# Value bias seeded by ScalarE, and one of four softmax sums a chunk prepared on GpSimd

## The chip, the cores and the metric

The kernel runs on one core of one Trainium2 chip. The metric is the device time of one execution in microseconds (us). The kernel before takes 356.97 us, the median of three runs (356.93 to 358.93).

## The reference, cut to what matters

The input x has 128 sequences of 64 tokens with 128 features, ctx a context of the same shape. First comes a cross-attention with 16 heads of 8 features, whose softmax goes over the heads, not over the keys:

```python
k = split_heads(ctx @ Wk.T + bk); q = split_heads(layernorm(x) @ Wq.T + bq)
v = split_heads(ctx @ Wv.T + bv)                 # [B, 16, S, 8]
score = einsum("bhij,bhkj->bhik", k, q) / sqrt(8)
attn = softmax(score, axis=1)                    # over the 16 heads
out = einsum("bhik,bhij->bhjk", attn, v)
x = x + merge(out) @ Wo.T + bo
x = x + ffn(layernorm(x))                        # three blocks of two dequantised layers, with low-rank parts
```

For each pair of a key and a query, then, 16 exponentials are summed and each is divided by the sum.

## The kernel before, in words

The 8192 tokens make 16 chunks of 512 tokens; a chunk is 8 sequences, in four pairs of two (p = 0 to 3). The cross-attention of all chunks runs first (some 225 us), the feed-forward phase behind it, with the first of its steps laid between the last chunks. The order on each engine is written out by hand; chunks 2 to 11 are a loop of two chunks a turn, the others are unrolled. Engines meet only through semaphores, and each engine works strictly in its own written order.

For each pair the work goes like this:

- TensorE, `scores` (L1441): 16 small products into `score_ps0` or `score_ps1`, turn about: 16 heads x 64 queries for the keys of two sequences. It signals `s_scores`.
- VectorE, `negmax` (L840): the negative maximum over the heads, 128x64 from 128x1024.
- TensorE, the shift (L1590): two products of 128x512 that add this maximum to the scores.
- ScalarE, `probs` (L1156): the exponentials of 128x1024, signalled by `s_exp`.
- VectorE, `zsum` (L858): the sum over the 16 heads, then `rz` (L861), its reciprocal.
- GpSimd, `probs` (L527): the exponentials times the reciprocal, in place, signalled by `s_probs`. There are four buffers `probs0` to `probs3`, one for each pair of a chunk, each with 8 bands of 64 x 2: the bands are the head pairs.
- TensorE, `att_ps` (L1647): 32 products of the weights with the block-diagonal values `v_diag`. Pair p of a chunk is used two quarters after its scores are shifted: pairs 0 and 1 in the quarters p = 2 and p = 3 of the same chunk, pairs 2 and 3 in p = 0 and p = 1 of the next.

On TensorE a quarter p begins with the scores of pair p+1, then comes the shift of pair p, then one piece of the projections for a later chunk (p=0: context and input turned, L1453 and L1459; p=1: queries, L1465 and their remainder L1485; p=2: keys, L1471 and L1491; p=3: the values of the next chunk, `project_v`, L1478), a part of the output projection (L1429) and the product with the weights. So the scores of pair 2 open quarter p=1.

`project_v` begins with `bias_rows` (L1413, `head_major=True`), a product of 128x512 that writes the value bias into the PSUM bank `work0`; the four value products (two records each) are added to it. ScalarE copies the result to `v_diag` (L1075).

GpSimd also computes, in quarter p=1 between the weights of pair 0 and of pair 1, the variance and its root for the input norm three chunks on (`input_variance`, L489 to L495, and `input_scale`, L476). VectorE computes the statistics for it (L618) in quarter p=1 behind the maximum of pair 1, and adds the attention's output to x (L774) in quarter p=3.

Of the kernel before, what the change touches and what calls it, by code (L numbers as in the profile page):

```python
# [9 lines left out]
ALU = mybir.AluOpType  # L10
ACT = mybir.ActivationFunctionType
AX_X = mybir.AxisListType.X
AX_XY = mybir.AxisListType.XY
# [6 lines left out]
P = 128  # L20
# [3 lines left out]
ADJ = 2  # L24
# [41 lines left out]
def build(nc, x, ctx_in, wk, bk, wq, bq, wv, bv, wo, bo, qw, qs, qb, la, lb, gamma, beta, out):  # L66
# [7 lines left out]
    with ExitStack() as es:  # L74
        def sb(name, shape, dt=F32):
            return es.enter_context(nc.sbuf_tensor(name, shape, dt))
# [4 lines left out]
        def sem(name):  # L81
            return es.enter_context(nc.semaphore(name))
# [17 lines left out]
        wq_c = sb("wq_c", [P, P])  # L100
        w_t = {k: sb("w_t_" + k, [P, P]) for k in "qkv"}
        wo_split = sb("wo_split", [P, 2, 2, P])
        wo_t = sb("wo_t", [P, 2, 2, P])
        cols = sb("cols", [P, NROWS])
        cols_h = sb("cols_h", [P, NROWS])
# [34 lines left out]
        v_diag = [sb(f"v_diag{i}", [P, PPC * HEADS * 32]) for i in range(2)]  # L140
        negmax = [sb(f"negmax{i}", [P, SEQ], BF16) for i in range(2)]
        probs = [sb(f"probs{i}", [P, BANDS, SEQ, ADJ]) for i in range(4)]
        zsum = [sb(f"zsum{i}", [P, SEQ]) for i in range(2)]
        rz = [sb(f"rz{i}", [P, SEQ]) for i in range(4)]
        att_t = [sb(f"att_t{i}", [P, 2, CHUNK // 2]) for i in range(2)]
# [72 lines left out]
        h_stack, h_k_stack = sem("h_stack"), sem("h_k_stack")  # L218
        h_q_out = [sem(f"h_q_out{u}") for u in range(2)]
        s_v_ps = sem("s_v_ps")  # L220
        s_v = sem("s_v")
        s_att_t = sem("s_att_t")
        s_wo = sem("s_wo")
# [3 lines left out]
        s_negmax = sem("s_negmax")  # L227
        s_shifted = sem("s_shifted")
        s_exp = sem("s_exp")
        s_zsum = sem("s_zsum")  # L230
        s_rz = sem("s_rz")
        s_probs = sem("s_probs")
# [20 lines left out]
        def live(c):  # L253

            return not isinstance(c, int) or 0 <= c < NCHUNK

        def some(count):

            return not isinstance(count, int) or count > 0
# [23 lines left out]
        def moments_slot(c):  # L283

            return 2 if isinstance(c, int) and c == 0 else 1

        def later(t):

# [177 lines left out]
        def _(pool):  # L466
# [18 lines left out]
            def input_variance(k):  # L485
# [10 lines left out]
                pool.wait_ge(s_aggr, 3 * k - 6)  # L496
                input_scale()

            def clear(tensor, done):

                for i in range(4):
                    ins = nc.gpsimd.memset(tensor[:, 512 * i:512 * (i + 1)], 0.0)
                ins.then_inc(done, 1)
# [13 lines left out]
            def chunk(c, par, half):  # L517
                for p in range(PPC):
                    n = PPC * c + p
                    mc = c - (p == 0)  # L520
                    if live(mc):
                        m = n - 1

                        pool.wait_ge(s_rz, m + 1)
                        e = probs[(p - 1) % 4]
                        by_query = rz[(p - 1) % 4][:, :].unsqueeze(1).unsqueeze(3)
                        nc.gpsimd.tensor_tensor(e[:, :, :, :], e[:, :, :, :],  # L527
                                                by_query.broadcast_to([P, BANDS, SEQ, ADJ]),
                                                ALU.mult).then_inc(s_probs, 1)
                    if p == moments_slot(c) and live(c + 3):  # L530
                        input_variance(c + 3)
                    input_part(X_VARIANCES, c, p, input_variances)
                    input_part(X_SCALES, c, p, input_scales)
                    early_steps("POOL", c, p, step)
# [80 lines left out]
        def _(dve):  # L615
# [214 lines left out]
                residual_columns()  # L830

            def chunk(c, par, half):
                for p in range(PPC):
                    n = PPC * c + p
                    if live(c):

                        dve.wait_ge(s_scores, n + 1)
                        if some(n - 1):
                            dve.wait_ge(s_shifted, n - 1)
                        nc.vector.tensor_reduce(negmax[p % 2][:, :],  # L840
                                                score_ps[p % 2][:, :].rearrange("p (h k) -> p k h", k=SEQ),
                                                AX_X, ALU.max, negate=True).then_inc(s_negmax, 1)
                    if p == moments_slot(c) and live(c + 3):
                        if not isinstance(c, int) or c + 3 >= 4:
                            dve.wait_ge(s_xnext[1 - par], 16 * (half + par))
                        else:
                            dve.wait_ge(s_xin[3], 16)
                        dve.wait_ge(s_rstd, c + 3)
                        input_stats_of(c + 3)
                    if p == 3 and isinstance(c, int) and c == NCHUNK - 2:  # L850
                        add_attention(c - 2)
                    mc = c - (p == 0)
                    if live(mc):

                        m = n - 1
                        q = (p - 1) % 2
                        dve.wait_ge(s_exp, m + 1)
                        nc.vector.tensor_reduce(zsum[q][:, :], probs[(p - 1) % 4][:, :, :, :].rearrange("p u k s -> p k u s"),  # L858
                                                AX_XY, ALU.add).then_inc(s_zsum, 1)
                        dve.wait_ge(s_zsum, m + 1)  # L860
                        nc.vector.reciprocal(rz[(p - 1) % 4][:, :], zsum[q][:, :]).then_inc(s_rz, 1)  # L861
                    if p == 3 and live(c - 2) and not (isinstance(c, int) and c == NCHUNK - 2):
                        add_attention(c - 2)
                    if isinstance(c, int) and (c, p) == (1, 0):
                        dve.wait_ge(s_res, 1)
                    input_part(X_STATS, c, p, input_stats_ahead)
                    early_steps("DVE", c, p, step)
                    if isinstance(c, int) and (c, p) == (NCHUNK, 0):
                        third_step()
                    if isinstance(c, int) and (c, p) == (NCHUNK, 3):  # L870
                        step_stats(4, 0)
                    if isinstance(c, int) and (c, p) == (NCHUNK + 1, 3):
                        step_sums(4, 0)
# [119 lines left out]
        def _(act):  # L993
# [12 lines left out]
            def early_layers():  # L1006

                act.wait_ge(s_lint_ps, 1)
                nc.scalar.activation(lin_t[:, 1:3, :].rearrange("p l d -> p (l d)"), att_ps[:, P:3 * P],
                                     ACT.Copy).then_inc(s_lint, 1)  # L1010
# [54 lines left out]
            def k_low(k, par):  # L1065
# [2 lines left out]
                nc.scalar.activation(parts[par][:, 1, 1, :], work1[:, :], ACT.Identity,  # L1068
                                     bias=cols_h[:, ROW_BK:ROW_BK + 1]).then_inc(s_k_lo, 1)

            def value_blocks(k, par, src=work0):

                for b in range(2):
                    dst = v_diag[par][SEQ * b:SEQ * (b + 1), :].rearrange("p (u a e) -> p u a e", a=4, e=16)
                    ins = nc.scalar.activation(  # L1075
                        dst[:, :, 0:4:3, DH * b:DH * (b + 1)],
                        src[SEQ * b:SEQ * (b + 1), :].rearrange("p (u s j) -> p u s j", s=2, j=DH), ACT.Copy)
                ins.then_inc(s_v, 1)
# [71 lines left out]
            def chunk(c, par, half):  # L1150
# [29 lines left out]
                if live(c + 2):  # L1180
                    q_high(c + 2, par)
                    if isinstance(c, int) and c == 0:
                        early_layers()
                    q_low(c + 2, par)
                if isinstance(c, int) and c == 0:
# [17 lines left out]
                if live(c + 2):  # L1203
                    k_high(c + 2, par)
                    if isinstance(c, int) and c == 0:
                        one_layer(4, 2)
                    k_low(c + 2, par)
                for u in range(2):
                    input_part(X_SCALED[u], c, 2, lambda t, u=u: input_scaled(t, u))
                early_steps("ACT", c, 2, step)  # L1210
# [140 lines left out]
        def _(pe):  # L1351
# [121 lines left out]

            def project_v(par, dst=work0):

                bias_rows(dst[:, :], 0, head_major=True)
                for q in range(PPC):
                    ins = nc.tensor.matmul(dst[:, TILE * q:TILE * (q + 1)], ctx_tr[par][:, TILE * q:TILE * (q + 1)],  # L1478
                                           w_t["v"][:, :], start=False, stop=True, skip_group_check=True)
                ins.then_inc(s_v_ps, 1)  # L1480
# [84 lines left out]
            def chunk(c, par, half):  # L1565
                for p in range(PPC):
# [15 lines left out]
                    if isinstance(c, int) and c == 0 and p == 0:  # L1582
                        pe.wait_ge(s_pick, 2 + len(BIAS_ROWS))
                        pe.wait_ge(s_split, 7)
                        project_v(0, wo_ps)

                    if live(c):
# [13 lines left out]
                    if p == 2 and live(c + 2):  # L1601
                        project_k(c + 2, par)
                    if p == 3 and live(c + 1):
                        if live(c + 2):
                            pe.wait_ge(s_q_lo, c + 3)
                        else:
                            pe.wait_ge(s_v, c + 1)
                        project_v(1 - par)

                    if isinstance(c, int) and (c, p) == (NCHUNK - 1, 3):  # L1610
# [278 lines left out]
```

## Time and profile before

| what | value |
|---|---|
| median of three runs | 356.97 us |
| profiled execution | 357.28 us, of it the span 355.5 us |
| granted TensorE clock, mean | 1.000 of full speed |
| TensorE busy | 340.4 us (96%) |
| VectorE busy | 325.9 us (92%) |
| ScalarE busy | 289.9 us (82%) |
| GpSimd busy | 266.1 us (75%) |

The span is the time from the first to the last instruction; the time outside it is the start and end of the program. Busy times are those of instructions alone. The profile names each instruction by its line (L527), its engine (PE is TensorE, PEld its weight loads, DVE VectorE, ACT ScalarE, POOL GpSimd) and the buffers that it writes and reads, without their numbers. Matmuls overlap each other, and their ends are modelled.

### The profile page before, as it was taken

To read this page: it belongs to the slowest core of one execution; us is meant where nothing else is said; L and a number is where in the kernel's file an instruction comes from. 1 tells how busy PE (TensorE), PEld (TensorE's weight loads), DVE (VectorE), ACT (ScalarE), POOL (GpSimd) and SP (SyncE) were. 2 spreads that over 40 slices of the span, in tenths; PEclk is the share of its full clock that TensorE was granted. 3 is DMA by queue.
4 is the path that set the end of the run, shared out by engine and by line. 5 is a ranking of instruction groups with operands and counts; after the bars stand their busy time and mean duration, and the time that the engine had idled before them with its cause. 6 is when DMAs were issued, how large, how long until landed. Compare 5 with 4: busy or idle time off the path is not lost.

```text
span 355.5 us, 13101 instructions
## 1 busy us (share of the span) xinstructions
PE 340.4 (96%) x4807; PEld 255.3 (72%) x4807; DVE 325.9 (92%) x818; ACT 289.9 (82%) x597; POOL 266.1 (75%) x283
## 2 busy tenths in 40 slices
PE   8979999999999999999999989999999999999995
PEld 7445477667667667766766767867888888888874
DVE  7879999999999999999999999978999999988774
ACT  4678888888878878888887878588989999999982
POOL 6537888877977987987799898878777778774231
PEclk9999999999999999999999999999999999999999
DMA  7989566659548746854944500000100001110112
GB/s 199 237 254 258 153 191 207 190 140 264 173 131 228 202 137 192 229 163 139 266 137 126 158 4 2 2 2 2 32 30 30 30 30 48 43 32 30 44 47 89
DMA packets 54530, 43.29 MB, mean 122 GB/s; under 512 B 4624, under 2 KB 48608, under 8 KB 54496
## 3 DMA queue, kind: packets, MB, share of 16 engines
q1 hardware_dynamic: 53920, 42.31, 41.0%
q10 hardware_dynamic: 576, 0.53, 0.5%
q8 instruction: 21, 0.34, 0.4%
q14 instruction: 13, 0.11, 0.1%
HBM read 26.05 MB, written 16.78 MB: 120 GB/s over the span
## 4 chain that ended last, share of the span: by engine, by line
PE 67%; POOL 10%; DVE 9%; ACT 4%; issue 4%; DMA 4%; SPq 1%; DVEq 0%; POOLq 0%; ACTq 0%
PE score_ps L1690 9%; POOL probs L527 7%; PE att_ps L1647 7%; PE score_ps L1590 6%; PE wo_ps L1429 5%; PE score_ps L1441 4%; PE score_ps L1793 3%; PE work L1465 3%; PE work L1786 3%; PE att_ps L1793 3%; PE work L1478 3%; PE work L1471 2%; PE score_ps L1684 2%; DVE st L884 2%; DVE zsum L858 2%
## 5 line engine op out<-in xcount | busy, mean ns | idle before, releaser
L527 POOL TENSOR_TENSOR probs<-probs,rz 128x1024 f32<-128x1024 f32 x64 | 136.3, 2140 | 27.9 <-DVE rz L861 27.8
L570 POOL TENSOR_TENSOR rs<-ve,minus_half 128x4 f32<-128x4 f32 (+1 forms) x47 | 55.6, 1183 | 33.7 <-DVE ve L786 24.3
L858 DVE TENSOR_REDUCE zsum<-probs 128x64 f32<-128x1024 f32 x64 | 77.4, 1209 | 2.5 <-ACT probs L1156 2.5
L1156 ACT ACTIVATE probs<-score_ps 128x1024 f32<-128x1024 f32 x64 | 65.6, 1025 | 13.0 <-PE score_ps L1590 12.2
L840 DVE TENSOR_REDUCE negmax<-score_ps 128x64 bf16<-128x1024 f32 x64 | 75.1, 1175 | 1.1 <-PE score_ps L1441 1.1
L1429 PEld LDWEIGHTS wo_ps<-wo_t,att_t 128*128 128x128 f32 x256 | 37.0, 191 | 13.4 <-issue 12.0
L1647 PE MATMUL att_ps<-probs,v_diag 128*32 128x64 f32 x2048 | 43.3, 224 | 1.2 <-POOL probs L527 0.8
L1252 ACT ACTIVATE z<-score_ps,rs 128x128 f32<-128x128 f32 x152 | 43.5, 382 | 1.1 <-POOL rs L570 1.1
L1690 PEld LDWEIGHTS score_ps<-lin_t,h 128*128 128x128 f32 x304 | 36.9, 191 | 9.9 <-DVE h L937 6.8
L1690 PE MATMUL score_ps<-lin_t,h 128*128 128x128 f32 x304 | 39.6, 278 | 1.3 <-DVE h L937 0.8
L1647 PEld LDWEIGHTS att_ps<-probs,v_diag 128*32 128x32 f32 x2048 | 32.8, 108 | 11.1 <-POOL probs L527 2.8
L1590 PE MATMUL score_ps<-negmax,ident_bf 128*128 128x512 bf16 x128 | 38.7, 384 | 1.3 <-DVE negmax L840 1.2
L1429 PE MATMUL wo_ps<-wo_t,att_t 128*128 128x128 f32 x256 | 38.3, 275 | 0.0
L861 DVE RECIPROCAL rz<-zsum 128x64 f32<-128x64 f32 x64 | 35.4, 553 | 2.2
L884 DVE BATCH_NORM_STATS2 st<-score_ps 128x6 f32<-128x128 f32 x152 | 33.8, 284 | 3.5 <-PE score_ps L1690 2.5
L1441 PE MATMUL score_ps<-q_stack,k_stack 64*64 64x128 f16 x1024 | 26.5, 222 | 2.5 <-DMA q_stack<-q_parts 1.6
L1441 PEld LDWEIGHTS score_ps<-q_stack,k_stack 64*64 64x64 f16 x1024 | 16.6, 106 | 13.9 <-issue 11.2
L476 POOL TENSOR_TENSOR half_rstd<-veps,minus_half 128x4 f32<-128x4 f32 x16 | 16.5, 1031 | 5.8 <-DVE veps L630 2.4
L1023 ACT ACTIVATE xln<-x_all,half_rstd 128x128 f32 (+1 forms) x60 | 19.0, 391 | 0.4 <-POOL half_rstd L476 0.4
L1786 PEld LDWEIGHTS work<-lin_t,g 128*128 128x128 f32 x104 | 13.7, 192 | 6.2 <-issue 6.2
L1263 ACT ACTIVATE g<-score_ps,cols 128x512 f32<-128x512 f32 x21 | 16.8, 798 | 1.4 <-PE score_ps L1684 1.4
L1075 ACT ACTIVATE v_diag<-work 64x512 f32<-64x512 f32 x30 | 17.6, 585 | 0.3
(275 smaller groups left out, 692.7 us busy)
## 6 DMA issues: line engine op xcount, KB each, us to landing
q_parts<-parts SPq DMA_DIRECT2D x15, 512.0 KB, 3.6
k_stack<-k_parts SPq DMA_DIRECT2D x30, 256.0 KB, 3.4
q_stack<-q_parts SPq DMA_DIRECT2D x60, 128.0 KB, 3.3
x_all<-in_x SPq DMA_DIRECT2D x16, 256.0 KB, 3.9
ctx_sb<-in_ctx SPq DMA_DIRECT2D x16, 256.0 KB, 3.7
k_parts<-parts SPq DMA_DIRECT2D x16, 256.0 KB, 3.0
out<-x_all SPq DMA_DIRECT2D x15, 256.0 KB, 2.3
q_parts<-parts SPq DMA_DIRECT2D x4, 128.0 KB, 2.3
```

What stands on the lines that cost most here:

```text
L527: nc.gpsimd.tensor_tensor(e[:, :, :, :], e[:, :, :, :], by_query.broadcast_to([P, BANDS, SEQ, ADJ]), ALU.mult).then_inc(s_probs, 1)
L570: nc.gpsimd.tensor_tensor(rs2[v][:, lo:hi], ve2[v][:, lo:hi], minus_half[:, lo:hi], ALU.pow).then_inc(p_rs[v], 1)
L840: nc.vector.tensor_reduce(negmax[p % 2][:, :], score_ps[p % 2][:, :].rearrange("p (h k) -> p k h", k=SEQ), AX_X, ALU.max, negate=True).the ...
L858: nc.vector.tensor_reduce(zsum[q][:, :], probs[(p - 1) % 4][:, :, :, :].rearrange("p u k s -> p k u s"), AX_XY, ALU.add).then_inc(s_zsum, 1)
L884: ins = nc.vector.bn_stats(st2[v][:, lo + i, :], src[:, TILE * i:TILE * (i + 1)])
L1156: nc.scalar.activation(probs[p][:, :, :, :], score_ps[p % 2][:, :].rearrange("p (u s k) -> p u k s", s=ADJ, k=SEQ), ACT.Exp, scale=SCALE). ...
L1252: ins = nc.scalar.activation(z[v][0][:, t, :], src[:, TILE * t:TILE * (t + 1)], ACT.Copy, scale=rs2[v][:, lo + t:lo + t + 1])
L1429: ins = nc.tensor.matmul(wo_ps[:, TILE * t:TILE * (t + 1)], att[:, o, TILE * u:TILE * (u + 1)], wo_t[:, o, b, :], start=False, stop=o == 1 ...
L1441: ins = nc.tensor.matmul(score_ps[mp % 2][SEQ * b:SEQ * (b + 1), c0:c0 + 2 * SEQ], k_stack[mb][half_rows, grp, k0:k0 + SEQ], q_stack[mb][h ...
L1590: ins = nc.tensor.matmul(score_ps[p % 2][:, CHUNK * o:CHUNK * (o + 1)], ident_bf[:, :], negmax[p % 2][:, :].unsqueeze(1).broadcast_to([P, ...
L1647: ins = nc.tensor.matmul(att_ps[32 * grp:32 * (grp + 1), c0:c0 + SEQ], v_diag[mb][:, v0:v0 + 32], probs[mp][:, band(hd), :, hd % ADJ], sta ...
L1690: ins = nc.tensor.matmul(dst[:, TILE * t:TILE * (t + 1)], hk[:, TILE * t:TILE * (t + 1)], lin_t[:, 2 * v - 2, :], start=v == 1 and t == 0, ...
```

## The change

Two things change.

The value bias: ScalarE reads the bias row once into SBUF (`value_row`, in chunk 0, from a product of 128 columns that TensorE puts into a free part of `att_ps`), and from then on copies it in each chunk, four times side by side, into `work0` (`value_seed`), between the two parts of the keys. `project_v` adds its products to that; the bias product goes, but for chunk 0's values, which are written to `wo_ps`.

The sum of pair 0: in chunks 1 to 12 GpSimd divides the weights of pair 3 of the chunk before in two halves of four bands, and between the halves adds the upper eight heads of pair 0's exponentials to the lower eight (`half_sum`, 128x512). VectorE sums eight instead of sixteen values for this pair, and takes the maximum of pair 2 ahead of this sum; in its old place that maximum is left out.

```diff
@@ -140,6 +141,7 @@
         probs = [sb(f"probs{i}", [P, BANDS, SEQ, ADJ]) for i in range(4)]
+        half_sum = sb("half_sum", [P, BANDS // 2, SEQ, ADJ])
@@ -283,6 +287,10 @@
+        def halved(c):
+
+            return not isinstance(c, int) or 1 <= c <= 12
@@ -496,6 +504,11 @@
+            def weigh(e, by_query, lo, hi):
+
+                return nc.gpsimd.tensor_tensor(e[:, lo:hi, :, :], e[:, lo:hi, :, :],
+                                               by_query.broadcast_to([P, hi - lo, SEQ, ADJ]), ALU.mult)
@@ -524,9 +537,14 @@
                         by_query = rz[(p - 1) % 4][:, :].unsqueeze(1).unsqueeze(3)
-                        nc.gpsimd.tensor_tensor(e[:, :, :, :], e[:, :, :, :],
-                                                by_query.broadcast_to([P, BANDS, SEQ, ADJ]),
-                                                ALU.mult).then_inc(s_probs, 1)
+                        if p == 0 and halved(c):
+                            weigh(e, by_query, 0, BANDS // 2)
+                            pool.wait_ge(s_exp, n + 1)
+                            nc.gpsimd.tensor_tensor(half_sum[:, :, :, :], probs[0][:, 0:BANDS // 2, :, :],
+                                                    probs[0][:, BANDS // 2:BANDS, :, :], ALU.add).then_inc(s_half, 1)
+                            weigh(e, by_query, BANDS // 2, BANDS).then_inc(s_probs, 1)
+                        else:
+                            weigh(e, by_query, 0, BANDS).then_inc(s_probs, 1)
@@ -830,16 +848,25 @@
+                def maxima(p):
+
+                    n = PPC * c + p
+                    dve.wait_ge(s_scores, n + 1)
+                    if some(n - 1):
+                        dve.wait_ge(s_shifted, n - 1)
+                    nc.vector.tensor_reduce(negmax[p % 2][:, :],
+                                            score_ps[p % 2][:, :].rearrange("p (h k) -> p k h", k=SEQ),
+                                            AX_X, ALU.max, negate=True).then_inc(s_negmax, 1)
+
+                def head_sums(q, src):
+
+                    nc.vector.tensor_reduce(zsum[q][:, :], src.rearrange("p u k s -> p k u s"), AX_XY,
+                                            ALU.add).then_inc(s_zsum, 1)
...
-                    if live(c):
...
+                    if live(c) and not (halved(c) and p == 2):
+                        maxima(p)
@@ -854,9 +881,13 @@
-                        dve.wait_ge(s_exp, m + 1)
-                        nc.vector.tensor_reduce(zsum[q][:, :], probs[(p - 1) % 4][:, :, :, :].rearrange("p u k s -> p k u s"),
-                                                AX_XY, ALU.add).then_inc(s_zsum, 1)
+                        if p == 1 and halved(c):
+                            maxima(2)
+                            dve.wait_ge(s_half, c)
+                            head_sums(q, half_sum[:, :, :, :])
+                        else:
+                            dve.wait_ge(s_exp, m + 1)
+                            head_sums(q, probs[(p - 1) % 4][:, :, :, :])
@@ -1067,6 +1098,22 @@
+            def value_bias():
+
+                act.wait_ge(s_value_row, 1)
+                nc.scalar.activation(value_row[:, :], att_ps[:, 0:P], ACT.Copy).then_inc(s_value_row, 1)
+
+            def value_seed(k):
+
+                if live(k + 1):
+                    act.wait_ge(s_q_lo, k + 2)
+                else:
+                    act.wait_ge(s_v, k)
+                if isinstance(k, int) and k == 1:
+                    act.wait_ge(s_value_row, 2)
+                nc.scalar.activation(work0[:, :].rearrange("p (q d) -> p q d", q=PPC),
+                                     value_row[:, :].unsqueeze(1).broadcast_to([P, PPC, P]), ACT.Copy).then_inc(s_v_seed, 1)
@@ -1204,7 +1252,10 @@
                     k_high(c + 2, par)
...
+                    value_seed(c + 1)
                     k_low(c + 2, par)
+                elif live(c + 1):
+                    value_seed(c + 1)
@@ -1473,7 +1524,6 @@
             def project_v(par, dst=work0):
 
-                bias_rows(dst[:, :], 0, head_major=True)
@@ -1582,6 +1632,9 @@
+                        nc.tensor.matmul(att_ps[:, 0:P], pick_row[:, 0, :], bias3_h[:, :], start=False, stop=True,
+                                         skip_group_check=True).then_inc(s_value_row, 1)
+                        bias_rows(wo_ps[:, :], 0, head_major=True)
                         project_v(0, wo_ps)
@@ -1601,10 +1654,7 @@
-                        if live(c + 2):
-                            pe.wait_ge(s_q_lo, c + 3)
-                        else:
-                            pe.wait_ge(s_v, c + 1)
+                        pe.wait_ge(s_v_seed, c + 1)
                         project_v(1 - par)
```

VectorE in the loop, quarter p=1 and the beginning of p=2 of one chunk, before. `stats` are those of a later chunk's input, `negmax0` is pair 2's maximum, `zsum0` and `rz0` belong to pair 0, `zsum1` to pair 1:

```order
L618 BN_STATS stats<-x_all 128x6
L858 TENSOR_REDUCE zsum0<-probs0 128x64
L861 RECIPROCAL rz0<-zsum0 128x64
L837 REGISTER_ALU
L840 TENSOR_REDUCE negmax0<-score_ps0 128x64
L858 TENSOR_REDUCE zsum1<-probs1 128x64
L861 RECIPROCAL rz1<-zsum1 128x64
```

The same place now:

```order
L636 BN_STATS stats<-x_all 128x6
L854 REGISTER_ALU
L857 TENSOR_REDUCE negmax0<-score_ps0 128x64
L863 TENSOR_REDUCE zsum0<-half_sum 128x64
L892 RECIPROCAL rz0<-zsum0 128x64
L863 TENSOR_REDUCE zsum1<-probs1 128x64
L892 RECIPROCAL rz1<-zsum1 128x64
```

Pair 2's maximum has moved ahead of pair 0's sum and reciprocal, and with it its wait for the scores of pair 2; the sum now reads `half_sum`.

GpSimd in the loop, from the weights of pair 3 to those of pair 0, before; the rows below them are the moments:

```order
L527 TENSOR_TENSOR probs3<-probs3,rz3 128x1024
L524 REGISTER_ALU
L527 TENSOR_TENSOR probs0<-probs0,rz0 128x1024
L487 REGISTER_ALU
L488 REGISTER_ALU
L489 TENSOR_TENSOR agg<-stats 128x4
```

And now:

```order
L509 TENSOR_TENSOR probs3<-probs3,rz3 128x512
L542 REGISTER_ALU
L543 TENSOR_TENSOR half_sum<-probs0 128x512
L509 TENSOR_TENSOR probs3<-probs3,rz3 128x512
L509 TENSOR_TENSOR probs0<-probs0,rz0 128x1024
L495 REGISTER_ALU
```

The addition stands between two halves of pair 3's weights. Pair 0, the moments and pair 1 follow each other as before.

## Rows read from the trace of the kernel before

**Rows 1.** The page: busy time, share of the span and instructions of each engine.

```profile
PE 340.4 (96%) x4807; PEld 255.3 (72%) x4807; DVE 325.9 (92%) x818; ACT 289.9 (82%) x597; POOL 266.1 (75%) x283
```

**Rows 2.** Window of chunk 6: us, busy PE, PEld, DVE, ACT, POOL; clock, DMA, GB/s.

```profile
101.15:113.80 12.65, 12.65 (x242) 8.87 (x242) 12.37 (x17) 10.42 (x17) 10.41 (x10) 1.00 0.65 186
```

**Rows 3.** The chain of waits in chunk 4: start us, us, what.

```profile
82.20 0.22 PE work L1413
```

**Rows 4.** TensorE in order of time, chunks 5 and 6: start us, us, instruction.

```profile
87.48 0.42 PE L1441 MATMUL score_ps<-q_stack,k_stack 64*64 64x128 f16 x16
...
94.61 0.38 PE L1413 MATMUL work<-bias_h,pick_row 128*128 128x512 bf16 x1
...
96.47 0.69 PE L1647 MATMUL att_ps<-probs,v_diag 128*32 128x64 f32 x32
...
97.58 0.61 PE L1590 MATMUL score_ps<-negmax,ident_bf 128*128 128x512 bf16 x2
...
100.20 0.42 PE L1441 MATMUL score_ps<-q_stack,k_stack 64*64 64x128 f16 x16
...
109.26 0.68 PE L1647 MATMUL att_ps<-probs,v_diag 128*32 128x64 f32 x32
...
112.85 0.42 PE L1441 MATMUL score_ps<-q_stack,k_stack 64*64 64x128 f16 x16
```

**Rows 5.** VectorE in order of time, chunk 5: pair 0, pair 2's maximum, pair 1.

```profile
87.28 1.20 DVE L858 TENSOR_REDUCE zsum<-probs 128x64 f32<-128x1024 f32 x1
88.52 0.55 DVE L861 RECIPROCAL rz<-zsum 128x64 f32<-128x64 f32 x1
88.99 1.16 DVE L840 TENSOR_REDUCE negmax<-score_ps 128x64 bf16<-128x1024 f32 x1
90.07 1.20 DVE L858 TENSOR_REDUCE zsum<-probs 128x64 f32<-128x1024 f32 x1
```

**Rows 6.** GpSimd in order of time, chunk 5: pair 0, then pairs 1 and 2.

```profile
89.15 2.14 POOL L527 TENSOR_TENSOR probs<-probs,rz 128x1024 f32<-128x1024 f32 x1 [1.41 <-DVE rz L861]
...
93.48 4.24 POOL L527 TENSOR_TENSOR probs<-probs,rz 128x1024 f32<-128x1024 f32 x2
```

**Rows 7.** Groups by form: form, count, busy us, mean ns, idle before; several stretches.

```profile
L594 POOL TENSOR_TENSOR z<-x_all,rs 128x512 f32<-128x512 f32 x13 | 13.5, 1040 | 0.0
...
L1293 ACT ACTIVATE score_ps<-seed 128x512 f32<-128x512 f32 x15 | 9.4, 624 | 0.0
...
L774 DVE TENSOR_TENSOR x_all<-wo_ps,x_all 128x512 f32<-128x512 f32 x2 | 1.3, 628 | 0.0
```

**Rows 8.** ScalarE in order of time, chunk 5: the two key copies.

```profile
92.74 0.70 ACT L1062 ACTIVATE parts<-work,cols_h 128x512 f16<-128x512 f32 x1
93.92 0.69 ACT L1068 ACTIVATE parts<-work,cols_h 128x512 f16<-128x512 f32 x1 [0.48 <-PE work L1491]
```

**Rows 9.** Order of time, two releases: TensorE to VectorE, GpSimd to TensorE.

```profile
233.99 1.13 PE L1690 MATMUL score_ps<-lin_t,h 128*128 128x128 f32 x8 [0.53 <-ACT lin_t L1015]
...
235.15 0.89 DVE L884 BATCH_NORM_STATS2 st<-score_ps 128x6 f32<-128x128 f32 x4 [0.65 <-PE score_ps L1690]
...
210.54 4.23 POOL L527 TENSOR_TENSOR probs<-probs,rz 128x1024 f32<-128x1024 f32 x2
...
212.72 0.69 PE L1647 MATMUL att_ps<-probs,v_diag 128*32 128x64 f32 x32 [0.84 <-POOL probs L527]
```

**Rows 10.** TensorE in order of time: pair 2's scores and pair 1's product, chunks 1, 12.

```profile
36.93 0.42 PE L1441 MATMUL score_ps<-q_stack,k_stack 64*64 64x128 f16 x16 [0.17 <-ACT probs L1156]
...
45.84 0.69 PE L1647 MATMUL att_ps<-probs,v_diag 128*32 128x64 f32 x32
...
176.11 0.42 PE L1441 MATMUL score_ps<-q_stack,k_stack 64*64 64x128 f16 x16
...
185.50 0.69 PE L1647 MATMUL att_ps<-probs,v_diag 128*32 128x64 f32 x32
```

**Rows 11.** TensorE in order of time, end of chunk 14: a shift that waits.

```profile
207.45 0.60 PE L1590 MATMUL score_ps<-negmax,ident_bf 128*128 128x512 bf16 x2 [0.54 <-DVE negmax L840]
```

More of the change, by code:

```diff
@@ L102, in build @@
         wo_split = sb("wo_split", [P, 2, 2, P])
+        value_row = sb("value_row", [P, P])
         wo_t = sb("wo_t", [P, 2, 2, P])
@@ L220, in build @@
         s_v_ps = sem("s_v_ps")
+        s_value_row, s_v_seed = sem("s_value_row"), sem("s_v_seed")
         s_v = sem("s_v")
@@ L229, in build @@
         s_exp = sem("s_exp")
+        s_half = sem("s_half")
         s_zsum = sem("s_zsum")
@@ L832, in chunk @@
             def chunk(c, par, half):
+                def maxima(p):
[9 more added lines that the diff above has]
+                                            ALU.add).then_inc(s_zsum, 1)
                 for p in range(PPC):
                     n = PPC * c + p
-                    if live(c):
[L837 to L842, printed above, removed]
+                    if live(c) and not (halved(c) and p == 2):
+                        maxima(p)
                     if p == moments_slot(c) and live(c + 3):
@@ L1182, in chunk @@
                     if isinstance(c, int) and c == 0:
+                        value_bias()
                         early_layers()
```

## The prediction

> **What bounds the kernel now.** I read the page first, then the window of a whole chunk, the chain of waits in another, and the order of time on each engine over chunks 5 and 6. The page says that no engine stands out: TensorE is busy 96% of the span and VectorE 92% [rows 1]. In chunk 6 TensorE is busy 12.65 of 12.65 us, VectorE 12.37, ScalarE and GpSimd 10.42 and 10.41, at the full granted clock, 2.4 GHz [rows 2]. The chain of waits runs through TensorE alone there, and the value bias product stands in it with 0.22 us [rows 3]. So TensorE sets the period, with VectorE some 0.3 us behind.
>
> The rest rests on distances, which I take on TensorE. Call S the end of the scores of pair 2 (start + 0.42 us). The product of pair 1's weights with the values, which ends the quarter p=3, is due 8.57 us after S in chunk 5 (96.47 - 87.90) and 8.64 in chunk 6 (109.26 - 100.62); from its start to the next S go 4.15 us (loop jump included) and 4.01 (113.27 - 109.26) [rows 4]. Together 12.72 and 12.65: two consecutive periods.
>
> GpSimd delivers pair 1's weights like this: reciprocal of pair 0 starts at 88.52 on VectorE, GpSimd weighs pair 0 from 89.15 (0.63 later), then computes the moments of a later chunk, then weighs pair 1 from 93.48 to 95.62 (half of 4.24) [rows 5, 6]. From 89.15 to 95.62 are 6.47 us. TensorE wants the result at 96.47, so 0.85 us are spare.
>
> **The change, part by part.**
>
> *TensorE, value bias.* One product of 0.22 us [rows 3] goes from each of 15 chunks. In chunk 0 there is one 128-column product more. Gain where TensorE bounds: 0.22 a chunk.
>
> *ScalarE, value seed.* One copy of 128x512 from SBUF into PSUM a chunk, 0.62 us by the seed copies of the later phase [rows 7]. It stands between the two key copies, where ScalarE now waits 0.48 us for the key remainder [rows 8]. So the low key part comes some 0.1 us later, and the seed is in PSUM near 94.1 (92.74 + 0.70 + 0.62), before TensorE begins on the values at 94.61 [rows 4]. Cost: 0. If the gap were gone, the exponential behind it would be up to 0.6 us late.
>
> *VectorE.* Pair 0's sum takes 8 x 64 elements instead of 16 x 64: the whole takes 1.20 us [rows 5]. No row shows the half. Below stands half of the whole, 0.60; VectorE's addition of 128x512 takes 0.63 [rows 7]; with the reduction's pattern I allow up to 0.75 and take 0.67, near the row of equal size. That frees 0.5 us a chunk. But the order moves: pair 2's maximum now stands ahead of pair 0's sum.
>
> *GpSimd.* The whole product of 2.14 us [rows 6] becomes two halves, and between them comes an addition of 128x512. Products of 128x512 take 1.04 [rows 7]: 2.08 + 1.04 = 3.12 instead of 2.14, so GpSimd's 10.4 become 11.4 of 12.7. As a share that fits. I take 1.04 for the addition; as bounds 0.5 (half of a 1.04) and 2.14. The addition needs pair 0's exponentials, whose shift TensorE ends 2.43 us before S (97.58 + 0.61 to 100.62 [rows 4]); with 0.1 to ScalarE, an exponential of 1.0, 0.1 to GpSimd and the addition it is done about 0.2 us before S. VectorE wants it 1.1 us after S. So the wait added on it costs nothing up to about 1.3 us more.
>
> *The new loop.* Pair 2's maximum cannot start before S. Behind it, in VectorE's own order, stand pair 0's sum and reciprocal, and for them waits GpSimd's whole row. After S:
> - to the start of the maximum: 0.03 us (a product ends at 235.12, VectorE starts at 235.15) [rows 9] to 0.08 (reciprocal ends 89.07, GpSimd starts 89.15 [rows 5, 6]); I take 0.05, near the row of VectorE itself
> - maximum to next start: 1.08 (88.99 to 90.07) [rows 5]
> - half sum 0.67, and 0.04 to the reciprocal as now (87.28 + 1.20 to 88.52): 0.71
> - reciprocal to GpSimd's start: 0.63
> - weigh pair 0, moments, weigh pair 1: 6.47
> - to TensorE: 0.05 (the first of the two products from 210.54 ends near 212.67, TensorE starts 212.72) [rows 9]
>
> Sum 8.99 us after S. TensorE's own way to that place is now 8.57 and 8.64, less the bias 8.35 and 8.42. It will stand still there some 0.6 us. And this does not pass: the next S comes 4.15 or 4.01 us behind that product [rows 4], so the loop closes, with 13.14 and 13.00 us. Against 12.72 and 12.65 that is +0.42 and +0.35 a chunk, with TensorE's saving already swallowed. Put otherwise: GpSimd begins pair 0 now 1.25 us after S (89.15 - 87.90), and would begin it 2.47 after S.
>
> *Sum.* Chunk 1: now 8.49 from S to the product (45.84 - 37.35) [rows 10], so +0.50. Chunks 2 to 11: five of each kind, 5 x 0.42 + 5 x 0.35 = 3.85. Chunk 12: now already 8.97 (185.50 - 176.53) [rows 10], because VectorE's statistics of the second phase come in; those start about 0.12 later, so +0.12. From chunk 13 VectorE and GpSimd have hardly a gap and TensorE waits for them (0.54 us for a maximum at 207.45 [rows 11]), so the two bias products that still fall away there win nothing, and GpSimd starts 1.2 us in arrear: I put +0.1. Together 0.50 + 3.85 + 0.12 + 0.10 = 4.57. The profiled execution took 357.28 us (span 355.5 and 1.8 around it), 0.3 over the median 356.97. So 361.85 in it, and 361.5 as the median.
>
> *A rule against this result.* The shares say that TensorE and VectorE are the fullest, at 96% and 92% [rows 1], and the change relieves both. The Trainium skill, "Perfetto Trace Analysis", section "Identifying the Most-Contended Engine", says to take the engine with the highest occupancy first (for TensorE it wants the weight loads' share instead of the matmuls', and then VectorE is first). By that rule this change should win: that is rival 1 below. The distances above say that a chain through all three engines becomes longer than any engine's row; whether it is so, no row of before can show.
>
> For the addition the skill's "GPSIMD Engine Reference", section 3.1, gives 2.6 cycles an element at 1.2 GHz for two inputs. By it 512 elements would be 1.1 us, an estimate, which would leave the sum as it is.
>
> **Rivals.**
>
> 1. *TensorE stays the bound* (the other side: faster). Then 12 chunks save 0.22 each: -2.6, 354.7 in the profiled execution, 354.3 as the median. For it: the busy shares, and 0.85 us spare behind GpSimd now. Against it: the delay of GpSimd's start is 1.22 us, and 0.85 less the 0.22 by which TensorE comes earlier are there to hide it. It decides where the way from S to the product gets under 8.4: the loop would have to be 0.6 us shorter than I make it.
> 2. *The loop bites, but is shorter.* The ends of matmuls are modelled, so the maximum could start 0.07 us earlier; the half sum could be 0.60, another 0.07; and while TensorE stands still, its queue could take in the loop jump, so that the 4.15 us in every second chunk become 4.01. That is 0.14 in 12 chunks and 0.14 in 5 more, 2.4 together: +2.2, 359.5 in the profiled execution, 359.2 as the median. For it speaks that each of these is possible at once; against it, that VectorE's row at 235.15 starts behind the modelled end and not before it [rows 9].
> 3. *GpSimd gets slower by the neighbour.* If its added work beside VectorE's reductions made each of its instructions 10% longer, 6.47 would be 7.1, and 12 chunks cost 7.6 more: 369. Against it: in chunk 5 the products have 2.14 and 2.12 us [rows 6], alone or beside VectorE's longest reductions.
>
> **How the numbers follow.** A measurement of this kernel tells about 1% from no change, 3.6 us. My forecast, 361.5, has 0.67, rival 1 has 0.10, rival 2 has 0.18, rival 3 has 0.05. The forecast's own range is 360.4 to 363.2 (0.03 to 0.08 at S is -0.2 and +0.4 over 12 chunks; the half sum between 0.60 and 0.75 is -0.8 and +1.0; the tail -0.1 to +0.5, and not all at one end). The whole range takes in rival 2 and leaves rival 1, rival 3 and the outer edges out: 358.8 to 363.8. Slower by over 1% (above 360.5): 0.60 of the forecast, 0.02 of rival 2 and rival 3, 0.67 together. Within 1%: 0.07 of the forecast, 0.16 of rival 2, and 0.06 of rival 1, whose 354.3 lies 0.7% under the median: 0.29. Faster by over 1% (under 353.4): the rest of rival 1, 0.04.
>
> **What would show it.** In the profile after: chunks 2 to 11 with a period near 13.07 us; on TensorE a repeated gap of some 0.6 us before the weights product, released by GpSimd's product; on VectorE a gap of about 1 us before pair 2's maximum, released by the scores; GpSimd starting pair 0 some 2.4 us after S; no gap of VectorE before the half sum; ScalarE's seed near 0.62 and no wait for it. Wrong would be the forecast if TensorE had no gap there and a period of 12.43, or if the gap's releaser were the seed or the addition.

## The result, and the profile after

The changed kernel takes 362.74 us (median of 4 runs, 362.21 to 363.36), the kernel before 356.95 in the runs beside it: ratio 1.0149, 95% interval 1.0111 to 1.0188. It is slower by 1.5%. The profiled execution took 362.78 us, 5.50 more than that of before.

The page of the changed kernel, busy time and two of its groups (line, engine, operation, count, busy, mean ns, idle time before and its releaser):

```profile
PE 338.2 (94%) x4793; PEld 253.9 (70%) x4793; DVE 321.4 (89%) x818; ACT 296.9 (82%) x613; POOL 282.2 (78%) x307
...
L857 DVE TENSOR_REDUCE negmax<-score_ps 128x64 bf16<-128x1024 f32 x64 | 76.2, 1192 | 12.4 <-PE score_ps L1492 12.3
...
L1697 PE MATMUL att_ps<-probs,v_diag 128*32 128x64 f32 x2048 | 43.3, 224 | 8.5 <-POOL probs L509 8.2
```

Against [rows 1] TensorE has 2.2 us less to do and VectorE 4.5 us less, and both are idle for a larger share of a longer span. The two groups say where: VectorE waits for scores before a maximum, TensorE for GpSimd's weights. The waits of the same kernel (engine, line waited for, us in all, times, longest) give the counts:

```profile
DVE negmax L857 <- PE score_ps L1492: 12.3, 15, 1.0
PE att_ps L1697 <- POOL probs L509: 8.2, 14, 0.8
DVE zsum L863 <- ACT probs L1203: 1.2, 3, 0.6
POOL half_sum L543 <- ACT probs L1203: 0.3, 1, 0.3
```

Of each of the first two about one a chunk. The third line is the sums on VectorE: they waited three times, for ScalarE, and never for the addition. So the addition is not what the loop waits for; it waited itself only once (the fourth line). Then TensorE in order of time (start us, us, instruction, idle before and its releaser): pair 1's product in the chunks 1, 2, 3, 5, 6 and 11 and the scores of pair 2 in 1, 4, 5 and 6; the scores at 99.37, those of pair 1 of chunk 6, are the first product behind the loop jump. They answer to [rows 4] and [rows 10].

```profile
36.60 0.42 PE L1492 MATMUL score_ps<-q_stack,k_stack 64*64 64x128 f16 x16
...
46.09 0.69 PE L1697 MATMUL att_ps<-probs,v_diag 128*32 128x64 f32 x32 [0.53 <-POOL probs L509]
59.16 0.68 PE L1697 MATMUL att_ps<-probs,v_diag 128*32 128x64 f32 x32 [0.56 <-POOL probs L509]
...
72.23 0.68 PE L1697 MATMUL att_ps<-probs,v_diag 128*32 128x64 f32 x32 [0.64 <-POOL probs L509]
...
75.97 0.42 PE L1492 MATMUL score_ps<-q_stack,k_stack 64*64 64x128 f16 x16
...
89.03 0.42 PE L1492 MATMUL score_ps<-q_stack,k_stack 64*64 64x128 f16 x16
...
98.51 0.68 PE L1697 MATMUL att_ps<-probs,v_diag 128*32 128x64 f32 x32 [0.64 <-POOL probs L509]
99.37 0.42 PE L1492 MATMUL score_ps<-q_stack,k_stack 64*64 64x128 f16 x16 [0.18 <-issue]
...
102.35 0.42 PE L1492 MATMUL score_ps<-q_stack,k_stack 64*64 64x128 f16 x16
...
111.81 0.68 PE L1697 MATMUL att_ps<-probs,v_diag 128*32 128x64 f32 x32 [0.54 <-POOL probs L509]
...
177.39 0.69 PE L1697 MATMUL att_ps<-probs,v_diag 128*32 128x64 f32 x32 [0.63 <-POOL probs L509]
```

The same gap stands before the same product in each of the chunks 1 to 11, 0.53 to 0.64 us. From S (89.03 + 0.42) to the product are 9.06 us, in chunk 6 (102.77 to 111.81) 9.04. From the product of chunk 1 to that of chunk 11 are 131.30 us, 13.13 a turn. Before, it was 45.84 [rows 10] to 172.54 in this row of the kernel before, so 126.70 us, 12.67 a turn:

```profile
172.54 0.68 PE L1647 MATMUL att_ps<-probs,v_diag 128*32 128x64 f32 x32
```

VectorE and GpSimd of the changed kernel over the same stretch of chunk 5; they answer to [rows 5] and [rows 6]:

```profile
89.50 1.23 DVE L857 TENSOR_REDUCE negmax<-score_ps 128x64 bf16<-128x1024 f32 x1 [0.97 <-PE score_ps L1492]
90.64 0.68 DVE L863 TENSOR_REDUCE zsum<-half_sum 128x64 f32<-128x512 f32 x1
91.36 0.55 DVE L892 RECIPROCAL rz<-zsum 128x64 f32<-128x64 f32 x1
```

```profile
87.46 1.17 POOL L509 TENSOR_TENSOR probs<-probs,rz 128x512 f32<-128x512 f32 x1
88.58 1.27 POOL L543 TENSOR_TENSOR half_sum<-probs 128x512 f32<-128x512 f32 x1
89.82 1.16 POOL L509 TENSOR_TENSOR probs<-probs,rz 128x512 f32<-128x512 f32 x1
91.99 2.14 POOL L509 TENSOR_TENSOR probs<-probs,rz 128x1024 f32<-128x1024 f32 x1 [1.02 <-DVE rz L892]
...
96.33 5.36 POOL L509 TENSOR_TENSOR probs<-probs,rz 128x1024 f32<-128x1024 f32 x3
```

Read the loop in these rows: S (the end of pair 2's scores) at 89.45, maximum 0.05 later, 1.14 to the half sum, 0.72 to the reciprocal, 0.63 to GpSimd at 91.99. Pair 1's weights begin at 96.33 and are done near 98.46 (6.47 behind 91.99, as before), TensorE starts 0.05 later, and 4.26 us on is the next S. These are the signs that the forecast named: the gap of 0.6, VectorE's wait of 1 us (0.97), GpSimd 2.54 us after S, a turn of 13.13 where it had 13.07. The addition ended near 89.85, 0.8 us before the half sum wanted it, and before the half sum VectorE has no gap.

### The profile page after: what moved, and what is told of

Same layout as the page of the kernel before. It is cut to its first block, busy times and chain, and to the rows that moved or that the text cites. A ratio compares the mean times of both kernels' runs of the same rounds, so it can differ in the third digit from the quotient of the medians.

```text
span 361.0 us, 13114 instructions
## 1 busy us (share of the span) xinstructions
PE 338.2 (94%) x4793; PEld 253.9 (70%) x4793; DVE 321.4 (89%) x818; ACT 296.9 (82%) x613; POOL 282.2 (78%) x307
## 4 chain that ended last, share of the span: by engine, by line
PE 33%; POOL 31%; issue 23%; DVE 6%; ACT 3%; DMA 2%; POOLq 1%; SPq 0%; ACTq 0%; DVEq 0%
POOL probs L509 20%; PE score_ps L1740 9%; POOL half_sum L543 4%; PE score_ps L1843 3%; PE work L1836 3%; PE att_ps L1843 3%; PE score_ps L1734 2%; DVE st L915 2%; PE wo_ps L1740 1%; PE att_ps L1734 1%; PE work L1734 1%; PE work L1826 1%; DMA k_stack<-k_parts 1%; POOL half_rstd L484 1%; ACT probs L1203 1%
## 5 line engine op out<-in xcount | busy, mean ns | idle before, releaser
L509 POOL TENSOR_TENSOR probs<-probs,rz 128x1024 f32<-128x1024 f32 (+1 forms) x76 | 137.9, 1829 | 16.8 <-DVE rz L892 16.7
L857 DVE TENSOR_REDUCE negmax<-score_ps 128x64 bf16<-128x1024 f32 x64 | 76.2, 1192 | 12.4 <-PE score_ps L1492 12.3
L863 DVE TENSOR_REDUCE zsum<-probs 128x64 f32<-128x1024 f32 x52 | 62.3, 1197 | 1.3 <-ACT probs L1203 1.2
```

Of the source, the lines that this page charges most:

```text
L509: return nc.gpsimd.tensor_tensor(e[:, lo:hi, :, :], e[:, lo:hi, :, :], by_query.broadcast_to([P, hi - lo, SEQ, ADJ]), ALU.mult)
L857: nc.vector.tensor_reduce(negmax[p % 2][:, :], score_ps[p % 2][:, :].rearrange("p (h k) -> p k h", k=SEQ), AX_X, ALU.max, negate=True).the ...
L863: nc.vector.tensor_reduce(zsum[q][:, :], src.rearrange("p u k s -> p k u s"), AX_XY, ALU.add).then_inc(s_zsum, 1)
```

## The experiments

The theory: pair 2's maximum, now ahead of pair 0's sum on VectorE, ties GpSimd's row to S, and GpSimd's row ties the next S: a loop over three engines of about 13.1 us, in which neither TensorE's nor VectorE's savings count. The rivals, by the letters of the expectations below: the seed on ScalarE costs the time (A), the two parts simply add up, a gain of TensorE and a larger loss (B), or GpSimd's added work itself costs it (C). A fourth, that the addition is what is waited for, is called D here.

**One part alone.** The bias alone:

```
 def halved(c):
-    return not isinstance(c, int) or 1 <= c <= 12
+    return False
```

> Only the value bias is seeded by ScalarE; sums and order on VectorE and GpSimd as before the change. My theory (the loop through pair 2's maximum, the half sum and GpSimd costs all of the loss): the loss is gone; TensorE has 12.43 us a chunk and VectorE some 12.5, so 355.0 (354.2 to 356.3). Rival A, the seed on ScalarE or the wait for it costs: 357 or more.

Measured: 355.48 us (355.25 to 355.70), ratio 0.9954 (0.9938 to 0.9971). The window of one turn of this kernel (stretch, its us, busy PE, PEld, DVE, ACT, POOL; clock, DMA, GB/s), to be held against [rows 2]:

```profile
99.51:111.95 12.44, 12.44 (x241) 8.78 (x240) 12.30 (x18) 10.91 (x18) 10.40 (x10) 1.00 0.64 186
```

TensorE is full again, in 12.44 us. So the seed on ScalarE costs nothing (A falls), and the bias edit by itself gains 1.5 us. At chunk 12 a part is given back:

```profile
182.58 0.38 PE L1464 MATMUL wo_ps<-bias,pick_row 128*128 128x512 bf16 x1 [0.79 <-DVE x_all L792]
```

Before, this wait for VectorE was 0.25 us; VectorE does not get faster when TensorE does. The reverse, everything but the bias (the product back on TensorE, the seed gone from ScalarE):

```
+bias_rows(dst[:, :], 0, head_major=True)
...
-value_seed(c + 1)
```

> Only pair 0's half sum and the maximum ahead of it; the bias product stays on TensorE. My theory: TensorE's 0.22 us a chunk stand in front of a place where it waits anyway, so the time is that of the whole change, 362.7 (362.0 to 363.4). Rival B, the two parts simply add up: the whole change less the saving of 2.6, so 365.3.

Measured: 362.54 us (362.31 to 363.63), ratio 1.0158 (1.0136 to 1.0179). With or without TensorE's 0.22 us a chunk the time is the same, and the gap shows who pays; TensorE of this kernel:

```profile
98.61 0.69 PE L1694 MATMUL att_ps<-probs,v_diag 128*32 128x64 f32 x32 [0.42 <-POOL probs L509]
```

0.42 us instead of 0.64: TensorE's product fills a part of its own gap. The period is set elsewhere, and B, which had 365.3, falls.

**The order alone, without any new work.** The kernel before, where in chunks 1 to 12 VectorE only does pair 2's maximum ahead of pair 0's full sum:

```
-if live(c):
+if live(c) and not (ahead(c) and p == 2):
     maxima(p)
...
+if p == 1 and ahead(c):
+    maxima(2)
 dve.wait_ge(s_exp, m + 1)
```

> The kernel before, with one edit: in chunks 1 to 12 VectorE takes pair 2's maximum ahead of pair 0's full sum of sixteen. No half sum, no addition on GpSimd, no seed. My theory: the same loop as in the changed kernel, longer by the full sum instead of the half (1.20 for 0.68, 0.52 us) in 12 chunks, so 362.6 + 6.2 = 368.8 (368.0 to 369.8). Rival C, the order is harmless and GpSimd's halves and addition are the cost: 357 to 358.

Measured: 368.72 us (368.58 to 368.88), ratio 1.0332 (1.0315 to 1.0349), 11.8 us more by a swap of two instructions that saves and adds nothing. In order of time in this kernel, VectorE and GpSimd:

```profile
105.32 1.23 DVE L843 TENSOR_REDUCE negmax<-score_ps 128x64 bf16<-128x1024 f32 x1 [0.97 <-PE score_ps L1451]
106.47 1.21 DVE L868 TENSOR_REDUCE zsum<-probs 128x64 f32<-128x1024 f32 x1
...
108.34 2.14 POOL L527 TENSOR_TENSOR probs<-probs,rz 128x1024 f32<-128x1024 f32 x1 [3.08 <-DVE rz L871]
```

GpSimd stands still 3.08 us before pair 0 (1.41 in [rows 6]). In the changed kernel the full sum's place is taken by the half sum, which shortens this same loop by 0.5 us (0.68 instead of 1.21): over 12 chunks that is 6.4 us, and between 368.72 and 362.74 lie 6.0. The half sum repairs a half of what its own order breaks.

**The work alone, without the order.** The changed kernel, in which GpSimd halves and adds, but VectorE keeps the order of before and sums all 16 heads; the half sum is computed and not used, and GpSimd waits for its own addition before it weighs pair 0:

```
-if live(c) and not (halved(c) and p == 2):
+if live(c):
     maxima(p)
...
-maxima(2)
-dve.wait_ge(s_half, c)
-head_sums(q, half_sum[:, :, :, :])
+dve.wait_ge(s_exp, m + 1)
+head_sums(q, probs[0][:, :, :, :])
```

> GpSimd halves its product and adds as in the change, but nobody uses the sum: VectorE sums sixteen heads in its old order. My theory: as e1 within 0.6 us, because 1.4 us more on GpSimd fit in its gap: 355.3. Rival C, GpSimd's load or its effect on VectorE costs: 359 or more.

Measured: 355.96 us (355.56 to 355.99), ratio 0.9962 (0.9948 to 0.9976). GpSimd's 1.5 us a chunk more (two halves and an addition, 3.60, for 2.14) cost 0.5 us in all against the bias alone (355.48). C falls.

**A dose in the loop, and outside.** 0.5 us of zeros that GpSimd writes to a buffer nobody reads, in chunks 1 to 12 of the changed kernel; once between pair 0's weights and the moments, once ahead of pair 0's weights (in the code p is one more than the pair that is weighed):

```
+if p == 1 and halved(c):
+    nc.gpsimd.memset(spare[:, :], 0.0)
```

> The changed kernel, and in chunks 1 to 12 GpSimd writes 128x512 zeros (a start-to-start time of 0.48 us) between the weights of pair 0 and the moments, inside the loop of my theory. Each of 12 turns should get longer by all of it: 362.7 + 5.8 = 368.5 (368.0 to 369.2). If GpSimd had slack there: under 364.

```
 weigh(e, by_query, BANDS // 2, BANDS).then_inc(s_probs, 1)
+nc.gpsimd.memset(spare[:, :], 0.0)
```

> The changed kernel, and the same 0.48 us of zeros on GpSimd in the same chunks, but between the second half of pair 3's weights and the weights of pair 0, where GpSimd waits 1.0 us for the reciprocal: outside the loop. My theory: 362.7 (362.2 to 363.3). Rival C, GpSimd's load as such costs: as much as with the dose inside, 368.

Measured: inside 367.79 us (367.50 to 367.95), ratio 1.0302 (1.0285 to 1.0319), 5.05 over the changed kernel; outside 362.84 (362.37 to 365.53, the latter one run of four), ratio 1.0191 (1.0151 to 1.0231), 0.1 over it by the medians. GpSimd of the first kernel and TensorE of it, then GpSimd of the second:

```profile
109.49 0.53 POOL L550 MEMSET spare<- 128x512 f32 x1
```

```profile
100.74 0.69 PE L1700 MATMUL att_ps<-probs,v_diag 128*32 128x64 f32 x32 [1.11 <-POOL probs L510]
```

```profile
103.99 0.52 POOL L547 MEMSET spare<- 128x512 f32 x1
105.21 2.14 POOL L510 TENSOR_TENSOR probs<-probs,rz 128x1024 f32<-128x1024 f32 x1 [0.70 <-DVE rz L894]
```

Inside, TensorE's gap grows from 0.64 to 1.11, and the way from S to the product from 9.06 to 9.53 in chunk 5. That is nearly all of the 0.48 us from the start of the zeros to the next start on GpSimd. From the first product to that of chunk 11 it is 0.44 a turn on average. I had expected all of it in all 12 chunks, 5.8 us, and 367.79 lies just under my range. Outside, GpSimd's own wait shrinks from 1.02 to 0.70, and pair 0's weights begin 2.53 us after S (102.68), where they began 2.54 after it; from S to the product it is still 9.05 to 9.07 us in the chunks 1 to 11. The same amount of work on the same engine is worth nine tenths of its length or nearly nothing, by the side of one semaphore on which it stands. The same dose in the kernel before, behind pair 0's weights:

```
+if p == 1 and (not isinstance(c, int) or 1 <= c <= 12):
+    nc.gpsimd.memset(spare[:, :], 0.0)
```

> The kernel before, with the same 0.48 us of zeros behind the weights of pair 0 in chunks 1 to 12. My theory: there GpSimd has 0.8 us to spare on this way, so nearly nothing: 357.3 (356.9 to 358.0); only chunk 12, where GpSimd has hardly a gap, may pay. If GpSimd's row bounded already before: 362.

Measured: 357.45 us (356.91 to 358.22, 10 runs), ratio 1.0019 (1.0009 to 1.0028). That is 0.6 us over the 356.88 beside it, small but clear of the noise, where the same dose cost 5.05 inside the loop. In the chunks 2 to 6 of this trace pair 1's product comes 8.57 to 8.65 us after S, for 8.56 to 8.64 before: the stretch had its slack.

**Out of the loop.** The changed kernel with pair 2's maximum back behind pair 0's half sum and reciprocal:

```
 if p == 1 and halved(c):
-    maxima(2)
     dve.wait_ge(s_half, c)
...
 nc.vector.reciprocal(...)
+if p == 1 and halved(c):
+    maxima(2)
```

> The whole change, but VectorE sums pair 0's eight first and takes pair 2's maximum behind its reciprocal, as before. My theory: S, the scores of pair 2, are no more in the way to GpSimd; the next loop is VectorE's half sum with GpSimd's own row, about 12.3 us, so TensorE bounds with 12.43 to 12.5: 354.8 (354.0 to 356.0). Rival C, GpSimd's larger load is the cost: stays over 361.

Measured: 358.79 us (358.56 to 359.00), ratio 1.0043 (1.0027 to 1.0060): 3.9 better than the change, and a miss by some 4 us of my forecast. VectorE and GpSimd of this kernel:

```profile
101.21 0.69 DVE L863 TENSOR_REDUCE zsum<-half_sum 128x64 f32<-128x512 f32 x1 [0.66 <-POOL half_sum L543]
...
110.89 0.55 DVE L891 RECIPROCAL rz<-zsum 128x64 f32<-128x64 f32 x1
...
113.95 0.69 DVE L863 TENSOR_REDUCE zsum<-half_sum 128x64 f32<-128x512 f32 x1 [0.65 <-POOL half_sum L543]
```

```profile
111.52 1.17 POOL L509 TENSOR_TENSOR probs<-probs,rz 128x512 f32<-128x512 f32 x1 [0.38 <-DVE rz L891]
112.65 1.26 POOL L543 TENSOR_TENSOR half_sum<-probs 128x512 f32<-128x512 f32 x1
```

Here is a second loop, of 12.74 us (101.21 to 113.95): half sum, the rest of VectorE's chunk to pair 3's reciprocal (10.23 us, to 111.44), the lower half of pair 3's weights, the addition, and the next half sum. I had counted GpSimd's own row only, and not that the addition stands behind a product which needs VectorE's last reciprocal. Rival D, wrong for the change as it was made, is right here: VectorE waits for the addition 0.65 to 0.67 us in every turn of the loop. To shorten that stretch, 2 of the 8 bands of pair 3 go ahead of the addition instead of 4:

```
-weigh(e, by_query, 0, BANDS // 2)
+weigh(e, by_query, 0, BANDS // 4)
...
-weigh(e, by_query, BANDS // 2, BANDS).then_inc(s_probs, 1)
+weigh(e, by_query, BANDS // 4, BANDS).then_inc(s_probs, 1)
```

> As e3 (VectorE sums pair 0's eight first), but GpSimd weighs only two of pair 3's eight bands ahead of the addition and six behind it; the work is the same. The theory from e3's trace: a second loop of 12.74 us, from the half sum through VectorE's row to pair 3's reciprocal (10.23), the first half of pair 3's weights (1.13) and the addition (1.26), bounds e3. With a quarter ahead, the addition starts when pair 0's exponentials are there, 0.35 us earlier, and the loop takes 12.4 us, so that TensorE bounds again with 12.44: 355.6 (354.8 to 356.6). If e3's loss lay in GpSimd's total work, it stays at 358.8.

Measured: 356.89 us (356.51 to 357.21, 11 runs), ratio 0.9995 (0.9983 to 1.0008). 1.9 us better, where I wanted 3.2; it lies above my range. GpSimd of this kernel:

```profile
110.55 0.67 POOL L509 TENSOR_TENSOR probs<-probs,rz 128x256 f32<-128x256 f32 x1 [0.21 <-DVE rz L891]
111.54 1.27 POOL L543 TENSOR_TENSOR half_sum<-probs 128x512 f32<-128x512 f32 x1 [0.32 <-ACT probs L1204]
112.77 3.77 POOL L509 TENSOR_TENSOR probs<-probs,rz 128x768 f32<-128x768 f32 x2
```

In this turn, and in ten in all, the addition now waits for ScalarE's exponentials instead; a turn takes 12.55 us on average, not the 12.4 that I had reckoned.

**The better version again**, measured beside the last one:

> e1 once more, on the same chip as e9, to compare the two: 355.5 (355.2 to 355.8). If e9 is the faster of the two, pair 0's half sum is worth something once it is out of the loops.

Measured: 355.44 us (355.04 to 355.61), ratio 0.9955 (0.9942 to 0.9969). The bias edit alone beats both kernels, by 0.45% and by 2.0% (355.44 against 362.74). It also beats the last version, 356.89, by 1.45 us: in no order that was tried did pair 0's half sum gain anything. At pair 1's product that version is 0.61 us behind this one in chunk 1 and 1.16 in chunk 11, so half of the difference is there before the loop begins. Which chain holds it was not settled.

## Why the prediction was right, and where its sizes were off

The forecast of 361.5 us and the measured 362.74 differ by 1.2, and the mechanism is the one named. Step by step:

- *The loop closes at S.* Right: the order alone costs 11.8 us, the order with the half sum 5.5 (362.54 against 357.03 beside it), a dose inside counts for nine tenths and one outside does not, and with the order put back 3.9 us return.
- *TensorE's saving is swallowed.* Right: 362.54 with the product, 362.74 without it.
- *The seed costs 0.* Right: 0.62 us in ScalarE's old gap, and the gain appears as soon as the order is left alone:

```profile
94.86 0.62 ACT L1115 ACTIVATE work<-value_row 128x512 f32<-128x512 f32 x1
```

- *GpSimd's added work costs nothing as long as it lies ahead of S + 1.1.* Right in effect, wrong in size: the halves take 1.16 and the addition 1.27 us, where 1.04 was taken for each; 3.60 instead of 3.12 a chunk. The path to it was wrong too: I had the addition wait for pair 0's exponentials and end 0.2 us before S. In chunk 5 it ended 0.40 after S, because GpSimd comes to it only through its own row (pairs 1 and 2 and the lower half of pair 3 without a gap, 5.36 us from 96.33 in the next round). By groups of one form, in the changed kernel:

```profile
L509 POOL TENSOR_TENSOR probs<-probs,rz 128x512 f32<-128x512 f32 x24 | 27.9, 1164 | 0.0
...
L543 POOL TENSOR_TENSOR half_sum<-probs 128x512 f32<-128x512 f32 x12 | 15.3, 1271 | 0.3 <-ACT probs L1203 0.3
```

Neither error showed here, with 0.8 us still to spare. Both did in my forecast for the version out of the loop, where the addition is in the chain.

- *The sum.* 4.57 us forecast, 5.50 in the profiled execution. On pair 1's product: chunk 1 was put at +0.50 and came at +0.25 (46.09 against 45.84), because I left out that S itself comes earlier there, by 0.33 us (36.60 + 0.42 against 37.35 [rows 10]). The ten turns to chunk 11 were put at +3.85 and came at +4.60 (131.30 - 126.70). The term that was too small is the way from S to the product: 8.99 in my sum, and 9.04 to 9.07 in each of these ten chunks, 0.67 us together. In it the maximum takes 1.14 to the next start, after a wait, for 1.08, and the half sum 0.72 to the reciprocal for 0.71. The way from the product to the next S added next to nothing: where the loop jump lies in it, it is 4.16 in chunk 3 (72.23 to 76.39), 4.26 in chunk 5 ("0.18 issue"), 4.15 in 7 and 9, for 4.13 to 4.19 in the same chunks before. The turn of chunk 12 came at +0.18 for +0.12:

```profile
189.78 0.38 PE L1464 MATMUL wo_ps<-bias,pick_row 128*128 128x512 bf16 x1 [0.61 <-DVE x_all L792]
...
190.53 0.69 PE L1697 MATMUL att_ps<-probs,v_diag 128*32 128x64 f32 x32
...
217.75 0.67 PE L1697 MATMUL att_ps<-probs,v_diag 128*32 128x64 f32 x32 [0.84 <-POOL probs L509]
...
238.96 1.13 PE L1740 MATMUL score_ps<-lin_t,h 128*128 128x128 f32 x8 [0.52 <-ACT lin_t L1046]
```

There, VectorE's addition to x is the releaser, and the product at 190.53 is 5.03 us behind that of before. At 217.75 it still is (212.72 [rows 9]), and in the first layers at 238.96 it is 4.97 (233.99 [rows 9]). So the tail of the attention, for which I had 0.10, added nothing, and the last 0.5 us come in the feed-forward phase, whose instructions the change leaves as they are; no wait of their own was found for them, and the runs of this kernel lie 1.15 us apart.

- *The rivals.* Rival 1, that TensorE stays the bound, fell for the change (354.3 for 362.74) and was right in its direction for the bias alone, which gained 1.5 us of its 2.6. Rival 2, the shorter loop, fell: the way from S to the product came out longer, and standing still on TensorE did not hide the loop jump (4.15 to 4.26 us where 4.01 would have been needed). Rival 3, GpSimd slower by a neighbour, fell: its products of 128x1024 have 2.14 us as before.

The rule against this result failed here. The Trainium skill, "Perfetto Trace Analysis", section "Identifying the Most-Contended Engine", says to optimize the engine with the highest occupancy first, and to judge TensorE by its use of the peak and by the share of its weight loads instead of the matmuls'. With weight loads at 72%, VectorE with 92% is first [rows 1]. The change took 4.5 us of work from VectorE and 2.2 from TensorE's matmuls, and the kernel became 1.5% slower. Of its two edits, the one that relieves VectorE is the one that loses, by its order, and the one that relieves TensorE gains.

For the addition, the Trainium skill's "GPSIMD Engine Reference", section 3.1, led to an estimate of 1.1 us. The trace has 1.27 for the addition, 1.16 for the halves and 1.04 [rows 7] for another product of 128x512: the estimate lies among them, 0.17 under the addition itself, and the measurements decide.

## What to carry to other kernels

An instruction that is moved ahead on an engine with a fixed order brings its wait along, and everything behind it inherits that wait; if one of those feeds back to what is waited for, a loop over several engines is closed, and where it is longer than each engine's own row, its length, not the busy share of any engine, is the period. Before such a move, write down the distances from that event round to itself, waits left out, and compare with the period. When the loop is opened, look for the next one at once: a helper instruction put in the middle of another engine's row (the addition here) is bound to all that stands ahead of it.

## What the runs showed of the hardware that I had not expected

- A GpSimd product cut in two is dearer: 2 x 1.16 = 2.33 us for the 2.14 of the whole. And equal shapes don't cost the same: 128x512 in fp32 with two inputs took 1.04 us (x times a broadcast scale, in the later phase), 1.16 (half of the weights, in place) or 1.27 (the addition of two halves of one buffer). What makes the difference was not tested.
- The jump at the end of a turn of the written loop costs TensorE some 0.15 us: 4.13 to 4.19 from the product to S where it lies between them, 3.99 to 4.01 where it does not. That TensorE had stood still for 0.64 us shortly before made no difference in three of four turns (4.15 and 4.16), and in the fourth it took 4.26; why is open.
- In the changed kernel, pair 2's maximum, which had waited for its scores, took 1.23 us in chunk 5 and 1.14 to the next start. Those that had not waited took 1.16 and 1.08, as in [rows 5], but the one right behind the addition to x took 1.21.
